# Layer 1's context values made in layer 0's output stage, key rotations on VectorE between layer 1's gate products, and another order of work in its cross attention

## The reference

```python
x = _layernorm(x + _L0_attn_ref(x, ...))        # a linear recurrence: s = s @ A.T + uB_t; y = s @ Cm.T + D
x = _layernorm(x + _L0_xattn_ref(x, ctx, ...))  # 12 heads of 64
x = _layernorm(x + _L0_ffn_ref(x, ...))         # quantized to int8-like steps
x = _layernorm(x + _L1_attn_ref(x, ...))        # projection, causal convolution of 4 taps, gate, output
x = _layernorm(x + _L1_xattn_ref(x, ctx, ctx, ...))   # 16 heads of 16, rotary q and k, bias on v
x = _layernorm(x + _L1_ffn_ref(x, ...))
# _L1_xattn_ref
q = apply_rope(x @ Wq.T + bq); k = apply_rope(ctx @ Wk.T + bk); v = ctx @ Wv.T + bv
out = softmax(q @ k.T * 16 ** -0.5) @ v
return out @ Wo.T + bo
```

## Time and profile before

| what | us |
|---|---|
| median of 3 runs (2594.41 to 2601.98) | 2595.38 |
| the profiled execution | 2594.83 |
| its span, first to last instruction | 2593.0 |
| busy in the span: PE / PEld | 2283.1 (88%) / 1789.3 (69%) |
| busy in the span: DVE / ACT / POOL | 1314.9 (51%) / 906.4 (35%) / 709.2 (27%) |
| mean granted TensorE clock | 0.947 of full |

### The profile page before, as it was taken

One profiled execution on the slowest core, in us unless ns is written; L12 is line 12 of the kernel. 1 busy time (PEld: TensorE's weight loads), 2 busy tenths in 40 slices (PEclk: granted clock), 3 DMA queues, 4 the chain that ended last, 5 costly groups with the idle time before them and its releaser, 6 DMA issues. The chain is left out here.

```text
span 2593.0 us, 48661 instructions
## 1 busy us (share of the span) xinstructions
PE 2283.1 (88%) x18360; PEld 1789.3 (69%) x18369; DVE 1314.9 (51%) x2768; ACT 906.4 (35%) x1591; POOL 709.2 (27%) x1096
## 2 busy tenths in 40 slices
PE   8869999787989899999979988976977989599992
PEld 4647777453567565899968866645865778399992
DVE  4466666598668421111157754553137887511114
ACT  2233333484356301111122224521225667122223
POOL 1722222235223100122212221211325633133332
PEclk9889999898989999999999998987988999799996
DMA  7500000100020100788710003012530000399994
GB/s 281 190 1 1 0 0 1 26 1 1 1 92 2 52 0 1 269 315 316 259 51 0 0 3 95 2 52 83 165 84 5 2 2 3 116 322 327 325 325 139
DMA packets 162728, 253.57 MB, mean 98 GB/s; under 512 B 17296, under 2 KB 123536, under 8 KB 162320
## 3 DMA queue, kind: packets, MB, share of 16 engines
q1 hardware_dynamic: 153360, 230.42, 25.8%
q0 software_dynamic: 9216, 21.06, 3.0%
HBM read 219.79 MB, written 31.13 MB: 97 GB/s over the span
## 5 line engine op out<-in xcount | busy, mean ns | idle before, releaser
L3516 PE MATMUL te_pU<-te_xsT,te_wu 128*128 128x128 f32 x1952 | 233.5, 276 | 1.5 <-DVE te_xsT L3609 1.5
L3516 PEld LDWEIGHTS te_pU<-te_xsT,te_wu 128*128 128x128 f32 x1952 | 231.1, 193 | 5.2 <-issue 2.1
L3537 PE MATMUL te_pY<-te_wd,te_hT 128*128 128x256 f32 x976 | 220.8, 379 | 0.0
L3537 PEld LDWEIGHTS te_pY<-te_wd,te_hT 128*128 128x128 f32 x976 | 180.7, 190 | 22.1
L1230 PE MATMUL x_pB<-early,x_xlT 128*128 128x384 f32 x376 | 133.4, 499 | 1.7 <-ACT x_xlT L1362 1.7
L3566 ACT ACTIVATE te_hT<-te_pU 128x512 f32<-128x512 f32 x78 | 46.6, 597 | 234.9 <-PE te_pU L3516 234.9
L2547 DVE TENSOR_REDUCE x_mx<-x_pR 128x8 f32<-128x1024 f32 x64 | 78.3, 1223 | 78.0 <-PE x_pR L2301 78.0
L3590 DVE COPY te_ys<-te_pY 128x256 f32<-128x256 f32 x61 | 25.9, 425 | 162.8 <-PE te_pY L3537 162.8
L3585 DVE TENSOR_TENSOR te_hT<-te_pU,te_sg 128x512 f32<-128x512 f32 x44 | 30.4, 692 | 147.5 <-ACT te_sg L3564 147.5
L3564 ACT ACTIVATE te_sg<-te_pG 128x512 f32<-128x512 f32 x44 | 26.3, 597 | 210.2 <-PE te_pG L3516 210.2
L1230 PEld LDWEIGHTS x_pB<-early,x_xlT 128*128 128x128 f32 x376 | 68.8, 193 | 43.1 <-issue 4.3
(11 more groups left out here) (669 smaller groups left out, 5627.1 us busy)
## 6 DMA issues: line engine op xcount, KB each, us to landing
te_wu<-in_L_ffn_w_upT SPq DMA_DIRECT2D x39, 1024.0 KB, 5.9
te_wd<-in_L_ffn_w_downT SPq DMA_DIRECT2D x39, 1024.0 KB, 5.8
te_wu<-in_L_ffn_up SPq DMA_DIRECT2D x22, 1024.0 KB, 4.9
te_wg<-in_L_ffn_gate SPq DMA_DIRECT2D x22, 1024.0 KB, 6.9
te_wd<-in_L_ffn_down SPq DMA_DIRECT2D x22, 1024.0 KB, 7.6
moe_first<-in_L_ffn_W SPq DMA_DIRECT2D x8, 1024.0 KB, 8.5
xs_slots<-zeros SPq DMA_DIRECT2D x1, 5120.0 KB, 15.6
ys_slots<-zeros SPq DMA_DIRECT2D x1, 5120.0 KB, 28.9
```

The source lines that it names most:

```text
L3516: ins = pe.matmul(out[g][:, m, :], w[:, k, bass.ts(PER * g + m, P)], xsT[:, k, :], start=(k == 0), stop=(k == KD - 1))
L3537: ins = pe.matmul(pY[u][:, 0, :], hT[:, k, :], wd[u][:, k, :], start=(k == 0), stop=(k == KH - 1))
```

## The change

- `spare` ([P, 16, 256]) is allocated ahead of layer 0. First it holds the gelu results `gl`, then, from yout on, layer 1's values. `Wv` is loaded with `Cm` and `Dt` (the wait goes from 32 to 48), no longer with `core.x1`.
- yout: eight `value_pair`s on PE (four products of 256 columns each) and eight copies of 128x512 by ACT, put between the outputs and behind them. POOL adds `Dt` in place in `core.X`, all four groups first.
- x0: `turn_back` is gone on PE and ACT, with its waits.
- a1: DVE does the whole rotation, 16 steps, in the places of `GAPS` behind `products`; POOL none.
- x1: no `value` on PE and no copy of it on ACT; POOL adds `bv` to the stored values. PE, ACT, DVE and POOL have a new order.
- a3: `keys(n+1)` goes ahead of `turn_output(n-2)`.

```diff
@@ Recurrence.request_output
+        sp.dma_start(self.wv[:], a["L1_xattn_WvT"].rearrange("(k p) n -> p k n", p=P)).then_inc(self.out_loaded, 16)
@@ l0_attn_inputs
-        gl = s.sb("gl", [P, NG, KD, GT])
+        gl = spare[:].rearrange("p b d -> p (b d)").rearrange("p (g k t) -> p g k t", g=NG, k=KD)
@@ l0_attn_out, POOL and PE (both: wait_ge(loaded, 48))
-                pool.tensor_tensor(xres[g % 2][:], core.X[:, G * g:G * (g + 1), :],
-                                   Dt[:].unsqueeze(1).to_broadcast([P, G, D]), ALU.add).then_inc(xres_ready, 1)
+                x = core.X[:, G * g:G * (g + 1), :]
+                pool.tensor_tensor(x, x, Dt[:].unsqueeze(1).to_broadcast([P, G, D]), ALU.add).then_inc(xres_ready, 1)
...
-            residual(0)
-            residual(1)
+            for g in range(NG):
+                residual(g)
             for g in range(NG):
                 root(g)
-                if g + 2 < NG:
-                    residual(g + 2)
...
+            def value_pair(v):
+                if v >= len(pV):
+                    pe.wait_ge(v_stored, v - len(pV) + 1)
+                for i in range(2):
+                    for k in range(KD):
+                        ins = pe.matmul(pV[v % len(pV)][:, i, :], core.CT[:, k, bass.ts(2 * v + i, P)], rec.wv[:, k, :],
+                                        start=(k == 0), stop=(k == KD - 1))
+                ins.then_inc(v_ready, 1)
+
+            value_pair(0)
+            output(0)
+            output(1)
+            value_pair(1)
+            output(2)
+            value_pair(2)
+            value_pair(3)
+            output(3)
+            for v in range(4, NB // 2):
+                value_pair(v)
@@ l0_attn_out, ACT
-            for g in range(NG):
-                states(g)
-            for g in range(NG):
-                normalize(g)
+            def store_pair(v):
+                act.wait_ge(v_ready, v + 1)
+                act.copy(values[:, 2 * v:2 * v + 2, :], pV[v % len(pV)][:]).then_inc(v_stored, 1)
...
+            states(0)
+            states(1)
+            store_pair(0)
+            states(2)
+            states(3)
+            normalize(0)
+            store_pair(1)
+            normalize(1)
+            store_pair(2)
+            store_pair(3)
+            normalize(2)
+            store_pair(4)
+            store_pair(5)
+            normalize(3)
+            store_pair(6)
+            store_pair(7)
@@ l0_xattn, PE turn
                 if one:
-                    if isinstance(n, int) and n == 1:
-                        pe.wait_ge(e_done[1], n)
-                    else:
-                        pe.wait_ge(xT_stored, n - 1)
+                    pe.wait_ge(e_done[1], n)
                 scores(1)
...
                 attend(1).then_inc(o_ready, 1)
-                if one:
-                    turn_back(n - 1)
@@ l1_attn, DVE products and rotations
+                    for n in GAPS.get((g, m), ()):
+                        rotate(n)
+
+            GAPS = {(1, 0): (0, 1), (1, 1): (2, 3), (1, 2): (4, 5), (2, 3): (6, 7, 8, 9),
+                    (3, 0): (10, 11), (3, 1): (12, 13), (3, 2): (14, 15)}
...
+            def rotate(n):
+                i, step = divmod(n, 4)
+                k = core.keys1[:, chunks[i][0], chunks[i][1]]
+                if step == 0:
+                    ins = dve.stream_shuffle(out=turned[:], in_=k, mask=swap)
+                elif step == 1:
+                    ins = dve.tensor_tensor(over_blocks(k), over_blocks(k), table(core.x1.cosT), ALU.mult)
+                elif step == 2:
+                    ins = dve.tensor_tensor(over_blocks(turned[:]), over_blocks(turned[:]), table(core.x1.sinT), ALU.mult)
+                else:
+                    ins = dve.tensor_tensor(k, k, turned[:], ALU.add)
+                rotations.then(ins)
@@ attention16, PE
             for n in TURNS:
                 before_first(n)
                 scores(n, 0)
+                if rope and live(n + 1):
+                    queries(n + 1)
                 if live(n - 2):
                     attend(n - 2)
-                if own(n + 1) or rope and live(n + 1):
+                if own(n + 1):
                     queries(n + 1)
-                if own(n - 4):
+                if own(n - 4) or rope and crossed(n - 4):
                     turn_back(n - 4)
                 before_second(n)
                 scores(n, 1)
+                if own(n + 1):
+                    keys(n + 1)
                 if own(n + 1) and live(n - 2):
                     turn_output(n - 2)
-                if own(n + 1):
-                    keys(n + 1)
...
                 if crossed(n - 3):
                     output(n - 3)
-                if crossed(n - 4):
+                if not rope and crossed(n - 4):
                     turn_back(n - 4)
@@ attention16, DVE
                 if live(n):
                     maximum(n, 0)
...
-                if crossed(n - 4):
+                if not rope and crossed(n - 4):
                     spread(n - 4)
...
+                if rope and crossed(n - 4):
+                    scaled(n - 4)
                 if rope and live(n + 1):
                     rotate(n + 1)
                 if live(n):
                     maximum(n, 1)
...
-                if crossed(n - 4):
+                if not rope and crossed(n - 4):
                     scaled(n - 4)
...
                 if crossed(n - 3):
                     residual(n - 3)
+                if rope and crossed(n - 3):
+                    spread(n - 3)
```

More of the change, by code:

```diff
@@ L186, in __init__ @@
         super().__init__(core, region, name)
-        self.wq, self.wv = (self.take(KD, D) for _ in range(2))
-        self.matrices = [(self.wq, wq), (self.wv, wv)]
+        self.wq = self.take(KD, D)
+        self.matrices = [(self.wq, wq)]
+        if wv:
+            self.wv = self.take(KD, D)
+            self.matrices.append((self.wv, wv))
         if wk:
@@ L928, in request, with l0_attn_out @@
         sp.dma_start(self.rows[:, self.FIRST:, :], ctx[:, self.FIRST:, :]).then_inc(self.rest_loaded, 16)
-def l0_attn_out(core, a, rec, S, J, NC):
+def l0_attn_out(core, a, rec, S, J, NC, values):
     with Stage(core, "yout") as s:
@@ L935, in l0_attn_out @@
         state = [s.sb(f"state{i}", [P, KD, GT]) for i in range(2)]
-        xres, r = ([s.sb(f"{n}{i}", [P, G, D]) for i in range(2)] for n in ("xres", "r"))
+        r = [s.sb(f"r{i}", [P, G, D]) for i in range(2)]
         stats, mv = ([s.sb(f"{n}{i}", [P, G, w]) for i in range(2)] for n, w in (("stats", 6), ("mv", 2)))
@@ L939, in l0_attn_out @@
         y = [s.ps(f"y{i}", [P, G, D]) for i in range(2)]
+        pV = [s.ps(f"pV{i}", [P, 2, D]) for i in range(4)]
+        v_ready, v_stored = s.sem("v_ready"), s.sem("v_stored")
         quantized = s.sem("quantized")
@@ L1864, in _ @@
             early.wait(pool)
[L1865 to L1878, removed]
-                rotations.then(pool.tensor_tensor(k, k, k2, ALU.add))
             tail.pool_residual(pool, 0, b_out[:])
             tail.pool_residual(pool, 1, b_out[:])
-            for i in range(len(chunks)):
-                rotate(i)
             for p in range(2 * NG):
@@ L2191, in move_v @@
                 out = V[b % len(V)][:, :, 0:DH]
-                if part(b).values is not None:
+                if part(b).values is not None and not part(b).bv:
                     ins = pool.tensor_copy(out, part(b).values[:, block_of(b), :].rearrange("p (h d) -> p h d", d=DH))
                 else:
-                    since(pool, v_copied, b)
-                    ins = pool.tensor_tensor(out, v32[:].rearrange("p (h d) -> p h d", d=DH),
+                    if part(b).values is None:
+                        since(pool, v_copied, b)
+                        row = v32[:]
+                    else:
+                        row = part(b).values[:, block_of(b), :]
+                    ins = pool.tensor_tensor(out, row.rearrange("p (h d) -> p h d", d=DH),
                                              part(b).early.bvt[:].rearrange("p (h d) -> p h d", d=DH), ALU.add)
@@ L2227, in _ @@
             for n in TURNS:
+                if rope and crossed(n - 4):
+                    root(n - 4)
                 if crossed(n - 3):
@@ L2631, in _, with l1_xattn @@
                     residual(n - 3)
-def l1_xattn(core, a, after):
-    attention16(core, a, "x1", [Attention(core.x1, bq=True, bv=True, bo=True, rope=True, keys=core.keys1)], after=[*after, core.a2])
+                if rope and crossed(n - 3):
+                    spread(n - 3)
+def l1_xattn(core, a, after, values):
+    attention16(core, a, "x1", [Attention(core.x1, bq=True, bv=True, bo=True, rope=True, keys=core.keys1, values=values)], after=[*after, core.a2])
 class MaskWeights(Early):
```

71 lines of the change are left out of this document (26 added, 45 removed).

## The result

The changed kernel takes 2602.16 us (median of 9, 2599.62 to 2603.70), the kernel before 2595.38 (median of 9): ratio 1.0024, 95% interval 1.0015 to 1.0033. It is 6.8 us slower; the forecast was 10 faster. The kernel before makes steps of this size by itself: in another group of 31 executions of it, 14 took 2598 to 2603 us, at a mean granted clock of 0.941 to 0.944, and 17 took 2592.8 to 2595.7 at 0.946 or 0.947, so only groups of runs can be compared here. The profiled execution has a span of 2601.9 us against 2593.0, so 8.9 more (it is the longest of the changed kernel's nine), and the stages can be set beside each other.

The account below looks back on a forecast made before the run. It took PE to bound x0, yout's chain its end, DVE then PE a1, and PE x1 before a DVE loop. Terms 2.4 - 5.3 - 9.5 + 2.4 + 0 = -10.0 gave 2584.8 us; 8 in 10: 2576 to 2592.

Parts of the forecast that it names:

- right, +2.4: yout: added PE products and ACT copies make the stage end later, +2.4 us, bounds +1 to +3.5.
- The clock fell ahead of x0's first products as taken: Start of x0: clock taken to fall in PE's idle 4.5 us, 0; if it stays up, -3.
- `turn_back` costs PE 0.38 us a turn, in 13 turns PE has no gap: x0: taking turn_back out of PE gives -4.9 us, -5.3 with the stage's end.
- PE needs the last product at 705: +0.6: a1's end: DVE, with rotation steps 10 to 15, ends near 705.7, PE needs it at 705, +0.6.
- by it the prediction put 0.9 on this place: a1: by the skill, steps 10 and 11 would wait for POOL's store of pair 5, +0.9 in the sum.
- The prediction's 20.3 us of added work on DVE: a1: 4 shuffles of 1.30 and 12 steps of 1.22 us, 0.04 each for their own wait.
- the turn, 7.70: x1's full turn: a loop through DVE sets 7.70 us, -0.24 a turn, -2.4 in ten.
- this comes at blocks 13 and 14, 2 x 2.4 less what overlaps, +4.1: x1's end: turn_back ahead of turn_normal on PE waits for spread, root and scaled, +4.1 us.
- Start and early turns were taken at +1 and -1.1: x1: start +1, since the clock may rise a turn later; two early turns fall from 7.76 to 7.2, -1.1.
- Rival 2: x1: new order costs more than it gives, +7 in place of +2.4, 2589.4 us; chance 0.22.
- the turn is right, 0: a3: the wait for the placed key could go, but a loop sums to the whole 8.1 us turn: 0.
- the highest, 2598.3: Rival 3, a1: a rotation step costs DVE 2.7 us, not 1.25, +13.5, giving 2598.3; chance 0.06.

Follow-up runs that it names:

- the two runs with earlier statistics: x0's key statistics taken a half earlier: in the changed kernel, 2594.57 us, ratio 0.9997; in the kernel before, turn_back kept, 2594.35 us, ratio 0.9993.
- the new gaps: Changed kernel with a1's rotation steps 6, 7 and 8 put behind products (2, 1) and (2, 2): 2598.55 us, ratio 1.0011.
- the old order without the value product: Changed kernel with x1 put back into its old order, values still from yout: 2595.88 us, ratio 0.9996.
- `x1_filler`: Changed kernel with two products per turn that nobody reads in x1's first three turns: 2600.83 us, ratio 1.0016.
- four turns filled: Changed kernel with four mends, plus unread products in x1's first four turns and ahead of its last turn_back: 2581.95 us, ratio 0.9944.

## Why the prediction was wrong, step by step

- **yout**: right, +2.4, by the mechanism told (1.6 to 2.4 in the nine profiles of kernels with this stage). The clock fell ahead of x0's first products as taken, though later; x0's first turns gained 0.8 by it.
- **x0**: the step "`turn_back` costs PE 0.38 us a turn, in 13 turns PE has no gap" failed. Six such transposes in the next row take 0.68 from start to start (319.42 to 320.10), so two should take 0.23; the other 0.15 was a wait. "Busy 220.00 of 220 us" hid it. With `turn_back` out, the key's chain (product, statistics 1.0, root, 1.08 of scaling) is what PE waits for, and the full turns gain nothing (mean 20.0). The 2.2 us won are in the first turns and behind the last key (0.8 and 2.2, less 0.8 that the turns between lost). Shown by the two runs with earlier statistics.
- **a1**: right up to the second gates (10.0 sooner). The step "PE needs the last product at 705: +0.6" was mis-sized: 2.35 us of wait, shown by the new gaps. DVE had hardly any idle time from 684 on; it came to `products(3, 0)` at 698.74, 104.6 us into the stage where 103.3 was counted, and step 10 took 1.63 us instead of 1.22 beside POOL's store (698.99 to 699.89). That last is the case of the Trainium skill (SBUF — State Buffer, Who interferes with whom): by it the prediction put 0.9 on this place, the trace shows 0.4. Behind the wait PE's clock was low in the last transposes (1.11 us instead of 0.66). The prediction's 20.3 us of added work on DVE are 20.5 by its own terms; its sum doesn't use them.
- **x1**: the turn, 7.70, was right to the hundredth; that PE's work doesn't set it is shown by the old order without the value product, that it is the loop through DVE was not tried by itself (the sum was 7.6, and the 0.1 added to it was an estimate). The end failed: "this comes at blocks 13 and 14, 2 x 2.4 less what overlaps, +4.1". It comes in all of the last turns: PE waits 1.12, 1.71, 2.85 and 2.46 us for `x_xn`, with two turned results and two output products near or behind a fallen clock (output product 2.08 us instead of 1.13). +7.5 instead of +4.1. Start and early turns were taken at +1 and -1.1 with the clock's rise as the danger; it rose in time, and fell again: +3.1. The step that failed there is that the value product was counted as work of PE and hardly as what fills its pauses: without it the first turns are long in the old order too. Rival 2 named the end and reached +7 for the whole stage; it was +9.1, of which the run with the old order leaves 3.9.
- **a3**: the turn is right, 0: the wait for the placed key went, one of 4.0 us for DVE took its place, and the turn stayed. The stage as a whole took 254.7 to 254.8 us in the four profiles with its old order, 255.2 here and 255.0 to 257.1 in the others with the new one, so the new order costs there rather than wins.
- **Behind the touched stages**: taken at 0, it was +4.9. 0.9 is in sh1's first 9 us, at the low clock (its logits 3.64 us, before 3.33). That x1's pauses alone brought this is not shown: with them gone the clock fell at 868.8, and these 9 us took 10.1. 0.9 is in layer 2's route logits (from 1715 us), where the stage waits for SP's loads and one issue takes 3.22 us that took 1.94; the kernels with values in yout have that stage at 8.3 to 8.5 us in every profile, the four without at 7.6. Most of the other 3.1 are 0.7 ahead of layer 2's mask, 0.9 in the expert choice behind the logits and 1.3 behind a3. The first comes and goes in both groups of kernels (0.0 to 1.0). From the logits to the end the changed kernel loses 3.1 us in all, and the other profiles with the values in yout agree: 2.9 to 3.8 in seven of them, 0.7 in `x1_filler`, against 0.1 at most in the three other profiles with the values in x1. So some 3 us behind the touched stages come with the change, a term that the forecast put at nothing. Which part brings them (the order of the loads, SP's slower issue, a3's order, which all nine share) was not tried and stays open.
- **Up to yout**: +1.3, untouched but for the extra load and the place of `gl`. yout begins between 111.6 and 113.8 us in the profiles of kernels with that code: scatter, no effect shown.

The sum of the misses in the profiles: 3.1 in x0, 2.5 in a1, 6.7 in x1, 6.6 elsewhere, from -10.0 to +8.9. The measured 2602.16 us lies above every case that the prediction named: the highest, 2598.3, asked for 2.7 us a rotation step, and the steps took 1.22 to 1.30, one of them 1.63.

## What to carry to other kernels

Before a short instruction is taken out of an engine that looks full, compare its start-to-start time with the same instruction elsewhere: what is more is a hidden wait, and the operand of the next instruction may become the bound at once. A new order is to be priced in its full turns and again in the first and last ones, where nothing overlaps: here the full turns gave 1.7 us and the end cost 7.5. Work taken out of an engine that isn't the bound leaves a pause, and a pause of PE can have two prices, its own time and the clock behind it: without the value product x1's first turns cost 3.1 us more, with 1.2 GHz for some 6.8 us behind a pause of 1.80.

## What the runs showed of the hardware

- The granted clock in x1's first turns is not settled by one pause. It fell at about 742.8, behind a pause of 1.80 us and ahead of one of 1.17; with the first filled it fell 9 us later, behind pauses of 0.84 and 1.17; with four turns filled it stayed up. The kernels with x1's own value products took 22.2, 24.1, 24.0 and 24.1 us for the same three distances, so these differ by 1.9 us with x1 unchanged.
- A wait of PE can be missing from the timeline: in the kernel before one of 0.15 us stood inside the 0.38 us of the pair before it and showed as no idle time, while the changed kernel's 0.23 and 0.32 us at the same place show.
- The issue of one load on SP took 1.94 or 1.95 us in the four profiles with the values in x1 and 3.09 to 3.60 in the nine with them in yout, and a stage's end waited for SP (timeline of SP, the changed kernel, then the kernel before):

```profile
1720.92 3.22 SPq L107 DMA_DIRECT2D early<-in_L_xattn_Wq  x1
```

```profile
1715.23 1.94 SPq L107 DMA_DIRECT2D early<-in_L_xattn_Wq  x1
```
